# Causal mask of the attention scores: from TensorE's products to additions on VectorE

## The chip, the cores and the metric

The kernel runs on one core of a Trainium2 chip. Its time is the device time of one execution in microseconds (us). The kernel before took 1857.26 us, the median of three executions (1856.35, 1857.26 and 1864.93 us).

The engines are TensorE (PE in the profile, with its weight loads as PEld), VectorE (DVE), ScalarE (ACT), GpSimd (POOL) and SyncE (SP, which issues the DMAs). TensorE writes its results to PSUM, which the kernel declares as 128 partitions of eight banks of 512 32-bit words.

## The reference, cut to what matters

The program is a small audio model: a patch embedding, causal attention, a mixture of four experts, a linear recurrence and a quantised feed-forward block, with a residual sum around each. The input is 8 batch elements of 376 tokens of 256 columns after the embedding. The change touches the attention alone:

```python
def _L0_attn_ref(x, Wq, Wk, Wv, Wo, bo):
    HEADS = 16
    DIM_HEAD = 64
    ...
    q = split_heads(x @ Wq)
    k = split_heads(x @ Wk)
    v = split_heads(x @ Wv)
    q = apply_rope(q)
    k = apply_rope(k)
    sim = jnp.einsum('bid,bjd->bij', q, k) * scale
    causal = jnp.tril(jnp.ones((t, t), dtype=bool))
    sim = jnp.where(causal[None], sim, -jnp.inf)
    attn = jax.nn.softmax(sim, axis=-1)
    out = jnp.einsum('bij,bjd->bid', attn, v)
    out = out.reshape(b, h, t, d).transpose(0, 2, 1, 3).reshape(b, t, h * d)
    return out @ Wo + bo
...
h = h + _L0_attn_ref(_layernorm(h, axis=-1), L0_attn_Wq, L0_attn_Wk, L0_attn_Wv, L0_attn_Wo, L0_attn_bo)
```

## The kernel before

The whole program is one launch with stages in blocks of their own: embedding (to about 82 us of the profile), attention (to about 940 us), then experts, recurrence and feed-forward. Each stage begins when all engines have left the one before, so what the attention stage takes longer or shorter moves everything behind it.

Attention works on one batch element after the other, and in each on eight pairs of heads. The 376 tokens are three tiles of rows: 0 and 1 with 128 rows, 2 with 120. Scores of tile i are computed only for the columns up to its own end (128, 256 and 376 columns), so a causal mask is needed only in the last block of each tile, on the diagonal. The scores of both heads of a pair lie in PSUM banks 0 and 1 (tiles 0 and 1) and 2 and 3 (tile 2). All products are made three times from a high and a low part of each factor.

The order of work on every engine is written out by hand, in the order of the code, and semaphores tie the engines together. One batch element is `begin` (the values v, and the output projection of the element before) and eight times `step`, one for each pair c. I call them the first to the eighth step of elements 0 to 7. In a step on TensorE (`step`, L736) come, in this order: turn of the even head, which transposes the probabilities and divides them by the row sum (L650); a projection for a later pair (L612); the scores of the next pair (L625 and L635); turn of the odd head; mix of the even head, probabilities times values (L667); a second projection; mix of the odd head. In the fourth to eighth step of elements 1 to 7 a piece of the routing of the element before is added (`route`, L727).

The mask on TensorE is L620 to L627: before the scores of a pair, for each tile, two halves and two heads, a product of a 64-row half of an identity matrix with the matching half of the mask table, in bf16. The sum is the mask block itself (-1e30 above the diagonal, 0 elsewhere), which opens the accumulation in PSUM; the score products then add to it (start=False).

What follows the scores on the other engines in a step:
- VectorE (`step`, L1137): turned_low of the even head (L1000, the low part of the transposed probabilities, which allows mix), a shuffle for the rotation of q or k (L977), `maxima` of the next pair (L979 to L986, negated row maxima of tiles 2, 0, 1, both heads at once), turned_low of the odd head, two `diagonals` (L988), a shuffle, out_low (L1005). In some steps routing work is added, `weigh` in the sixth, `choose` at the end of the seventh, `place_rows` in the eighth, and the addition of a bias to the residual at the end of the fifth.
- ScalarE (`step`, L872): turned_high of the even head (L832), a copy of the projection (L810), the exp of tile 2 of the even head, which waits for its maximum (L823), only then turned_high of the odd head, then the exps of tiles 0 and 1 and of the odd head, parts of q and k (L816), a copy, out_high. In the fourth and fifth step router_x (L857) stands behind turned_high of the odd head.
- GpSimd rotates q and k and makes their low part (L950, L952, L954, L923).

Mix of the odd head waits for the odd turned_low:

```python
pe.wait_ge(pt_ready, 16 * b + h + 1 + CR_PT)
```

and the scores of a pair wait until all exps of the pair before have read their banks (L619).

Of the kernel before, what the change touches and what calls it, by code (L numbers as in the profile page):

```python
# [19 lines left out]
BF16 = mybir.dt.bfloat16  # L20
# [377 lines left out]
def attention(nc, psum, h0_rows, x_dram, weights, a, consts, ident, x_slots, h_rows, onehot, where, shared, raw_w, w_in,  # L398
# [3 lines left out]
    with ctx:  # L402
# [25 lines left out]
        mask = sb("mask", [P, 2, P], BF16)  # L428
        ident_b = sb("ident_b", [P, 2, P], BF16)
        mask_f = sb("mask_f", [P, 2, P])  # L430
        ident_f = sb("ident_f", [P, 2, P])
# [41 lines left out]
        (tables_in, masks_made, resid_in, cleared, v_made, v_high, v_low, proj_made,  # L473
# [3 lines left out]
            "tables_in masks_made resid_in cleared v_made v_high v_low proj_made "  # L477
# [59 lines left out]
        with nc.Block(no_gpsimd_drain=True) as block:  # L537
            @block.sync
            def _(sp):
# [4 lines left out]
                sp.dma_start(mask_f[:], a["c_mask"]).then_inc(tables_in, 16)  # L544
                sp.dma_start(ident_f[:], a["c_ident_halves"]).then_inc(tables_in, 16)
# [36 lines left out]
            def _(pe):  # L582
# [34 lines left out]
                def scores(b, c):  # L617

                    pe.wait_ge(exp_made, 16 * b + 2 * c + CR_EXP)  # L619
                    for it in range(TILES):  # L620
                        ni = TILE_ROWS[it]
                        for half in range(2):
                            for par in range(2):
                                r = slice(HEAD * par, HEAD * (par + 1))
                                pe.matmul(score_bank(par, it)[:, P * it:P * it + ni], ident_b[r, half, 0:ni],  # L625
                                          mask[r, half, 0:ni], start=(it != 1 and half == 0), stop=False,
                                          skip_group_check=True)  # L627
                    pe.wait_ge(qk_ready, 16 * b + 2 * c + 2 + CR_QK)
                    for it in TILE_ORDER:
                        ni = TILE_ROWS[it]  # L630
                        nj = P * it + ni
                        for i, (hq, hk) in enumerate(three):
                            for par in range(2):
                                r = slice(HEAD * par, HEAD * (par + 1))
                                last = pe.matmul(score_bank(par, it), qk[hq][r, c % 2, 0, P * it:P * it + ni],  # L635
                                                 qk[hk][r, c % 2, 1, 0:nj], start=False, stop=(i == 2),
                                                 skip_group_check=True)
                        if it != 0:
                            last.then_inc(scores_made, 1)
# [145 lines left out]
                pe.wait_ge(masks_made, 2)  # L785
# [130 lines left out]
            def _(pool):  # L916
# [25 lines left out]
                pool.wait_ge(tables_in, 64)  # L942
# [21 lines left out]
            def _(dve):  # L964
# [14 lines left out]
                def maxima(b, c):  # L979
                    for it in TILE_ORDER:  # L980
                        ni = TILE_ROWS[it]
                        if it != 1:
                            dve.wait_ge(scores_made, 16 * b + 2 * c + (1 if it == 2 else 2) + CR_SCORES)
                        last = dve.tensor_reduce(neg_max[0:ni, :, it], both_scores(it), AX_X, ALU.max, negate=True)  # L984
# [183 lines left out]
                dve.wait_ge(tables_in, 64)  # L1168
                dve.tensor_copy(mask[:], mask_f[:]).then_inc(masks_made, 1)
                dve.tensor_copy(ident_b[:], ident_f[:]).then_inc(masks_made, 1)  # L1170
# [1091 lines left out]
def constants():  # L2262
# [24 lines left out]
    halves = lambda x: np.tile(x.reshape(2, HEAD, P).transpose(1, 0, 2), (2, 1, 1)).astype(np.float32)  # L2287
    return {"c_moe": moe, "c_ids": ids, "c_slots": slots, "c_before": before, "c_ident_halves": halves(np.eye(P)), "c_cos": cos, "c_sin": sin, "c_mask": halves(np.where(behind, NEG, 0.0)),
# [38 lines left out]
```

## Time and profile before

| | |
|---|---|
| median of three executions | 1857.26 us |
| the profiled execution | 1865.4 us |
| span in its profile | 1863.6 us |
| PE busy | 1553.8 us, 83% of the span |
| PEld busy | 1466.1 us, 79% |
| DVE busy | 1250.3 us, 67% |
| ACT busy | 993.4 us, 53% |
| POOL busy | 1005.9 us, 54% |
| mean granted TensorE clock | 0.915 of full speed |

The span runs from the first instruction of the profiled execution to its last, and the execution's own time is 1.8 us longer. Busy is the time in which an engine had at least one instruction under way; TensorE's matmuls are pipelined, so two that overlap do not count twice. A granted clock of 1.00 is TensorE's 2.4 GHz level, 0.50 its 1.2 GHz level. A line as L984 is line 984 of the kernel before; in the rows `expert_raw` is a piece of memory that several stages share, which in this stage holds the raw projections, the rotation table and the probabilities.

### The profile page before, as it was taken

What the parts mean: (1) busy time and instruction counts of PE and PEld (TensorE: products, weight loads), DVE (VectorE), ACT (ScalarE), POOL (GpSimd) and SP (SyncE); (2) the same over time, 40 slices, a digit from 0 to 9 for tenths busy, and PEclk for the clock granted to TensorE, in tenths of its full rate; (3) what the DMA queues carried; (4) which work ended last, traced back from release to release, by engine and by line L of the source; (5) the groups of instructions that cost most, each with busy time, mean ns of one, the idle gap of its engine ahead of it and who ended that gap; (6) DMA issues with size and microseconds to landing.
All of it is one profiled execution on the core that took longest, in us unless ns stands there. A gap on an engine that the chain in (4) does not pass through costs nothing. (4 is left out here: it accounts for less than half of the span.)

```text
span 1863.6 us, 31359 instructions
## 1 busy us (share of the span) xinstructions
PE 1553.8 (83%) x11301; PEld 1466.1 (79%) x11301; DVE 1250.3 (67%) x2526; ACT 993.4 (53%) x2138; POOL 1005.9 (54%) x814
## 2 busy tenths in 40 slices
PE   5389998989899999989759999999998846699229
PEld 4278998989898888989749999999997845598229
DVE  6547575766767676757535666666668749558896
ACT  5446564746556464747435455455554424349562
POOL 4368475776667575866346667767765633100000
PEclk8679998989899998989969999999999978799659
DMA  5590001000010101000046555555554431003223
GB/s 208 206 309 18 18 18 35 6 25 23 18 35 18 35 18 35 1 18 18 26 145 183 141 140 142 137 141 144 138 143 114 105 84 42 26 1 124 75 70 113
DMA packets 88242, 153.53 MB, mean 82 GB/s; under 512 B 8056, under 2 KB 65720, under 8 KB 87832
## 3 DMA queue, kind: packets, MB, share of 16 engines
q1 hardware_dynamic: 77576, 137.70, 23.8%
q0 software_dynamic: 10512, 13.83, 4.4%
q8 instruction: 90, 1.47, 0.3%
q14 instruction: 64, 0.52, 0.1%
HBM read 113.42 MB, written 51.45 MB: 88 GB/s over the span
## 5 line engine op out<-in xcount | busy, mean ns | idle before, releaser
L1523 POOL TENSOR_TENSOR expert_w_low<-expert_raw,expert_w_high 128x768 fp32r<-128x768 f32 x152 | 288.6, 1947 | 172.2 <-ACT expert_w_high L1348 167.1
L823 ACT ACTIVATE expert_raw<-psum,neg_max 120x376 f32<-120x376 f32 (+2 forms) x384 | 176.4, 482 | 140.6 <-DVE neg_max L984 140.5
L650 PE MATMUL psum<-diag,expert_raw 128*128 128x128 f32 (+2 forms) x1536 | 208.5, 288 | 26.5 <-DVE pt_low L1000 26.5
L650 PEld LDWEIGHTS psum<-diag,expert_raw 128*128 128x128 f32 (+2 forms) x1536 | 190.8, 199 | 33.2 <-issue 17.3
L923 POOL TENSOR_TENSOR qk_low<-rotated,qk_high 128x376 fp32r<-128x376 f32 x128 | 136.1, 1064 | 127.9 <-ACT qk_high L816 126.4
L1495 DVE TENSOR_TENSOR expert_act_low<-expert_act,expert_act_high 128x384 fp32r<-128x384 f32 x152 | 140.5, 924 | 79.9 <-ACT expert_act_high L1386 79.3
L1000 DVE TENSOR_TENSOR pt_low<-psum,pt_high 128x752 fp32r<-128x752 f32 x128 | 120.4, 940 | 106.3 <-ACT pt_high L832 106.1
L1386 ACT ACTIVATE expert_act_high<-expert_act 128x384 fp32r<-128x384 f32 x152 | 79.8, 525 | 205.5 <-DVE expert_act L1490 203.3
L950 POOL TENSOR_TENSOR rotated<-expert_raw 128x376 f32<-128x376 f32 x128 | 127.8, 999 | 94.9 <-ACT expert_raw L810 74.5
L1307 PE MATMUL psum<-slots_high,expert_w_high 128*128 128x384 f32 x608 | 159.6, 343 | 17.6 <-DVE expert_act L1490 16.5
L1307 PE MATMUL psum<-slots_low,expert_w_high 128*128 128x384 f32 x608 | 156.5, 338 | 0.0
L1307 PE MATMUL psum<-slots_high,expert_w_low 128*128 128x384 f32 x608 | 156.3, 338 | 0.0
L1318 PE MATMUL psum<-expert_w_high,expert_act_high 128*128 128x256 f32 x456 | 134.3, 295 | 11.7 <-ACT slot_out L1368 10.2
L952 POOL TENSOR_TENSOR expert_raw<-expert_raw,rope_sin 128x376 f32<-128x376 f32 x128 | 131.3, 1026 | 16.9 <-DVE expert_raw L977 16.9
L954 POOL TENSOR_TENSOR rotated<-rotated,expert_raw 128x376 f32<-128x376 f32 x128 | 130.9, 1023 | 10.0
L1348 ACT ACTIVATE expert_w_high<-expert_raw 128x768 fp32r<-128x768 f32 x152 | 126.5, 833 | 15.6 <-PEq L537 15.6
L1490 DVE TENSOR_TENSOR expert_act<-psum,silu 128x384 f32<-128x384 f32 x152 | 84.7, 557 | 67.3 <-ACT silu L1382 63.1
L1318 PE MATMUL psum<-expert_w_high,expert_act_low 128*128 128x256 f32 x456 | 128.4, 282 | 0.0
L1318 PE MATMUL psum<-expert_w_low,expert_act_high 128*128 128x256 f32 x456 | 128.4, 281 | 0.0
L832 ACT ACTIVATE pt_high<-psum 128x752 fp32r<-128x752 f32 x128 | 102.2, 798 | 47.1 <-PE psum L650 45.0
L667 PE MATMUL psum<-pt_high,v_high 128*128 128x376 f32 (+2 forms) x384 | 119.4, 311 | 3.8 <-DVE pt_low L1000 3.7
L1307 PEld LDWEIGHTS psum<-slots_high,expert_w_high 128*128 128x128 f32 x608 | 102.9, 191 | 24.3 <-issue 21.5
(294 smaller groups left out, 4451.5 us busy)
## 6 DMA issues: line engine op xcount, KB each, us to landing
expert_raw<-in_experts SPq DMA_DIRECT2D x152, 384.0 KB, 3.1
x_slots<-in_c_slots SPq DMA_DIRECT2D x4, 3168.0 KB, 28.6
slot_rows<-x_slots SPq DMA_DIRECT2D x19, 396.0 KB, 4.6
attn_x<-tok_xt SPq DMA_DIRECT2D x8, 752.0 KB, 4.0
x_parts<-attn_x SPq DMA_DIRECT2D x8, 752.0 KB, 4.6
up_spill<-held SPq DMA_DIRECT2D x5, 1128.0 KB, 5.0
held<-up_spill SPq DMA_DIRECT2D x5, 1128.0 KB, 6.6
patch<-in_patches SPq DMA_DIRECT2D x8, 376.0 KB, 8.1
```

What stands on the lines that cost most here:

```text
L650: last = pe.matmul(psum[0:nj, BANK_PT + bank, at:at + ni], probs[0:ni, h % 2, src:src + nj], diag[0:ni, h % 2, it, 0:ni], start=True, stop ...
L823: last = act.activation(probs[0:ni, h % 2, at:at + P * it + ni], score_bank(h % 2, it), ACT.Exp, bias=neg_max[0:ni, h % 2, it:it + 1], acc ...
L923: pool.tensor_tensor(qk[1][:, c % 2, k, :], rotated[:, k, :], qk[0][:, c % 2, k, :].bitcast(F32), ALU.subtract).then_inc(qk_ready, 1)
L950: pool.tensor_tensor(rotated[:, k, :], raw[:, k, :], cos[:], ALU.mult).then_inc(rope_made, 1)
L952: pool.tensor_tensor(swapped[:, k, :], swapped[:, k, :], sin[:], ALU.mult).then_inc(rope_made, 1)
L954: pool.tensor_tensor(rotated[:, k, :], rotated[:, k, :], swapped[:, k, :], ALU.add).then_inc(rot_made, 1)
L1000: dve.tensor_tensor(pt[1][:, h % 2, :, :], psum[:, BANK_PT:BANK_PT + 2, 0:TOK], pt[0][:, h % 2, :, :].bitcast(F32), ALU.subtract).then_inc ...
L1307: last = pe.matmul(psum[:, 2 * k + g % 2, 0:TILE_SLOTS], w[hw][:, f, at:at + P], xt[hx][:, i % 2, c, :], start=(n == c == 0), stop=(n == 2 ...
L1318: last = pe.matmul(psum[:, BANK_DOWN + s, 0:DIM], act_hl[ha][:, g % 2, P * s:P * (s + 1)], w[hw][:, f, 4 * P:4 * P + DIM], start=(n == f = ...
L1348: act.activation(w[0][:, g % RING, :], raw[:, g % RAW, :], ACT.Copy).then_inc(w_high, 1)
L1495: dve.tensor_tensor(act_hl[1][:, g % 2, :], act_f[:, g % 2, :], act_hl[0][:, g % 2, :].bitcast(F32), ALU.subtract).then_inc(low_made, 1)
L1523: pool.tensor_tensor(w[1][:, g % RING, :], raw[:, g % RAW, :], w[0][:, g % RING, :].bitcast(F32), ALU.subtract).then_inc(w_low, 1)
```

## The change

The masks leave TensorE. The two tables in bf16, the identity halves and the two casts that made them are gone; a table `causal` in 32-bit floats, 128 by 128 and once for each of two heads, is loaded in their place. The first score product of each tile now opens its accumulation (`start=(i == 0)`). On VectorE a new function `masked` adds the table to the diagonal block of each tile, in place in PSUM and for both heads at once: three TENSOR_TENSOR operations for each pair, over 2 x 120, 2 x 128 and 2 x 128 elements in a partition. `maxima` calls it first, and each maximum waits for its own tile's addition.

```diff
--- before.py
+++ after.py
@@ -425,10 +425,7 @@
         h = sb("attn_h", [P, T, DIM])
         rows = sb("x_rows", [P, T, ROW])
         xt = sb("router_x", [P, 2, TOK])
-        mask = sb("mask", [P, 2, P], BF16)
-        ident_b = sb("ident_b", [P, 2, P], BF16)
-        mask_f = sb("mask_f", [P, 2, P])
-        ident_f = sb("ident_f", [P, 2, P])
+        causal = sb("causal", [P, 2, P])
         holder = sb("holder", [P, 2 * PAIRS])
         stats = sb("row_stats", [P, T, 6])
         moments = sb("row_moments", [P, T, 2])
@@ -541,8 +538,7 @@
                     sp.dma_start(x[:, b, :, :, :].bitcast(F32), x_dram[:, :, :, tokens_of(b)]).then_inc(x_loaded[b], 16)
                 sp.dma_start(cos[:], a["c_cos"]).then_inc(tables_in, 16)
                 sp.dma_start(sin[:], a["c_sin"]).then_inc(tables_in, 16)
-                sp.dma_start(mask_f[:], a["c_mask"]).then_inc(tables_in, 16)
-                sp.dma_start(ident_f[:], a["c_ident_halves"]).then_inc(tables_in, 16)
+                sp.dma_start(causal[:], a["c_mask"]).then_inc(tables_in, 16)
                 sp.dma_start(bo[:], a["token_rows"][:, 3, :]).then_inc(params, 16)
                 sp.dma_start(w[:], a["L0_ffn_router_w"].rearrange("(c p) e -> p c e", p=P)).then_inc(params, 16)
                 sp.dma_start(bias[:], a["router_b"]).then_inc(params, 16)
@@ -617,14 +613,6 @@
                 def scores(b, c):
 
                     pe.wait_ge(exp_made, 16 * b + 2 * c + CR_EXP)
-                    for it in range(TILES):
-                        ni = TILE_ROWS[it]
-                        for half in range(2):
-                            for par in range(2):
-                                r = slice(HEAD * par, HEAD * (par + 1))
-                                pe.matmul(score_bank(par, it)[:, P * it:P * it + ni], ident_b[r, half, 0:ni],
-                                          mask[r, half, 0:ni], start=(it != 1 and half == 0), stop=False,
-                                          skip_group_check=True)
                     pe.wait_ge(qk_ready, 16 * b + 2 * c + 2 + CR_QK)
                     for it in TILE_ORDER:
                         ni = TILE_ROWS[it]
@@ -633,7 +621,7 @@
                             for par in range(2):
                                 r = slice(HEAD * par, HEAD * (par + 1))
                                 last = pe.matmul(score_bank(par, it), qk[hq][r, c % 2, 0, P * it:P * it + ni],
-                                                 qk[hk][r, c % 2, 1, 0:nj], start=False, stop=(i == 2),
+                                                 qk[hk][r, c % 2, 1, 0:nj], start=(i == 0), stop=(i == 2),
                                                  skip_group_check=True)
                         if it != 0:
                             last.then_inc(scores_made, 1)
@@ -782,7 +770,6 @@
 
                 for n in range(2 * LEAD):
                     project(0, n)
-                pe.wait_ge(masks_made, 2)
                 scores(0, 0)
                 pe.wait_ge(params, 16 * 7)
                 pe.wait_ge(routing, 2)
@@ -939,7 +926,7 @@
 
                 for part in range(2):
                     pool.memset(v[part].rearrange("p t c (k n) -> p (t c) k n", k=3)[:, :, 1, :].bitcast(F32), 0.0).then_inc(cleared, 1)
-                pool.wait_ge(tables_in, 64)
+                pool.wait_ge(tables_in, 48)
                 for b in range(BATCH):
                     for n in range(2 * PAIRS):
                         if n == 2 * LEAD and b >= 2:
@@ -976,11 +963,19 @@
                     dve.memset(holder[:, n % (2 * PAIRS):n % (2 * PAIRS) + 1], 0.0)
                     dve.stream_shuffle(swapped[:, n % 2, :], raw[:, n % 2, :], swap).then_inc(swap_made, 1)
 
-                def maxima(b, c):
+                def masked(b, c):
                     for it in TILE_ORDER:
                         ni = TILE_ROWS[it]
                         if it != 1:
                             dve.wait_ge(scores_made, 16 * b + 2 * c + (1 if it == 2 else 2) + CR_SCORES)
+                        block = both_scores(it)[:, :, P * it:P * it + ni]
+                        dve.tensor_tensor(block, block, causal[0:ni, :, 0:ni], ALU.add).then_inc(mask_added, 1)
+
+                def maxima(b, c):
+                    masked(b, c)
+                    for it in TILE_ORDER:
+                        ni = TILE_ROWS[it]
+                        dve.wait_ge(mask_added, 3 * (8 * b + c) + TILE_ORDER.index(it) + 1)
                         last = dve.tensor_reduce(neg_max[0:ni, :, it], both_scores(it), AX_X, ALU.max, negate=True)
                         if it != 0:
                             last.then_inc(max_made, 1)
@@ -1165,9 +1160,7 @@
                 dve.wait_ge(params, 16 * 7)
                 dve.tensor_copy(before[:], before_f[:]).then_inc(routing, 1)
                 dve.tensor_copy(base[:], const("region"))
-                dve.wait_ge(tables_in, 64)
-                dve.tensor_copy(mask[:], mask_f[:]).then_inc(masks_made, 1)
-                dve.tensor_copy(ident_b[:], ident_f[:]).then_inc(masks_made, 1)
+                dve.wait_ge(tables_in, 48)
                 for n in range(2 * LEAD):
                     swap_pairs(0, n)
                 maxima(0, 0)
...
-    halves = lambda x: np.tile(x.reshape(2, HEAD, P).transpose(1, 0, 2), (2, 1, 1)).astype(np.float32)
-    return {"c_moe": moe, "c_ids": ids, "c_slots": slots, "c_before": before, "c_ident_halves": halves(np.eye(P)), "c_cos": cos, "c_sin": sin, "c_mask": halves(np.where(behind, NEG, 0.0)),
+    return {"c_moe": moe, "c_ids": ids, "c_slots": slots, "c_before": before, "c_cos": cos, "c_sin": sin, "c_mask": np.stack([np.where(behind, NEG, 0.0)] * 2, axis=1).astype(np.float32),
```

The lines of the changed kernel lie up to 13 lower. On TensorE, around the scores of a pair in an ordinary step, this stood in the queue (psum<-mask,ident_b are the products of the mask; brackets name the semaphores that an instruction waits for):

```order
L612 MATMUL psum<-x_parts,L_attn_Wq_high 128x376 [waits raw_made]
L612 MATMUL psum<-x_parts,L_attn_Wq_high 128x376 x3
L612 MATMUL psum<-x_parts,L_attn_Wq_low 128x376 x2
L625 MATMUL psum<-mask,ident_b 128x128 [waits exp_made]
L625 MATMUL psum<-mask,ident_b 128x128 x7
L625 MATMUL psum<-mask,ident_b 120x120 x4
L635 MATMUL psum<-qk_high 120x376 [waits qk_ready]
```

And in the changed kernel:

```order
L608 MATMUL psum<-x_parts,L_attn_Wq_high 128x376 [waits raw_made]
L608 MATMUL psum<-x_parts,L_attn_Wq_high 128x376 x3
L608 MATMUL psum<-x_parts,L_attn_Wq_low 128x376 x2
L623 MATMUL psum<-qk_high 120x376 [waits qk_ready,exp_made]
L623 MATMUL psum<-qk_high 120x376
```

The twelve products are gone, and the first score product waits for both semaphores. On VectorE, from turned_low of the even head to turned_low of the odd head, the queue before was:

```order
L1000 TENSOR_TENSOR pt_low<-psum,pt_high 128x752 [waits pt_high]
L976 MEMSET holder 128x1 [waits raw_made]
L977 STREAM_SHUFFLE expert_raw<-expert_raw 128x376
L984 TENSOR_REDUCE neg_max<-psum 120x2 [waits scores_made]
L984 TENSOR_REDUCE neg_max<-psum 128x2 [waits scores_made]
L984 TENSOR_REDUCE neg_max<-psum 128x2
L1000 TENSOR_TENSOR pt_low<-psum,pt_high 128x752 [waits pt_high]
```

And in the changed kernel:

```order
L995 TENSOR_TENSOR pt_low<-psum,pt_high 128x752 [waits pt_high]
L963 MEMSET holder 128x1 [waits raw_made]
L964 STREAM_SHUFFLE expert_raw<-expert_raw 128x376
L972 TENSOR_TENSOR psum<-psum,causal 120x2x120 [waits scores_made]
L972 TENSOR_TENSOR psum<-psum,causal 128x2x128 [waits scores_made]
L972 TENSOR_TENSOR psum<-psum,causal 128x2x128
L979 TENSOR_REDUCE neg_max<-psum 120x2 [waits mask_added]
L979 TENSOR_REDUCE neg_max<-psum 128x2 [waits mask_added] x2
L995 TENSOR_TENSOR pt_low<-psum,pt_high 128x752 [waits pt_high]
```

Three additions stand ahead of the first maximum, and the second of them carries the wait for the scores of tiles 0 and 1, which before stood behind the first maximum. The queues of ScalarE and GpSimd hold the same instructions as before.

## Rows read from the trace of the kernel before

**Rows 1.** Windows view, attention stage: us, busy us (xcount) per engine, granted clock, DMA share, GB/s.

```profile
110.00:905.00 795.00, 742.97 (x6252) 696.99 (x6251) 538.82 (x1270) 467.33 (x1304) 541.11 (x536) 0.95 0.10 30
```

**Rows 2.** Groups by form, PE: the mask products: xcount | busy us, mean ns | idle.

```profile
L625 PE MATMUL psum<-mask,ident_b 64*128 64x128 bf16 x512 | 25.6, 220 | 0.0
...
L625 PE MATMUL psum<-mask,ident_b 64*120 64x120 bf16 x256 | 17.5, 215 | 0.0
```

**Rows 3.** Timeline, TensorE, an ordinary step: start us, us, what [idle before <-releaser].

```profile
142.81 0.59 PE L650 MATMUL psum<-diag,expert_raw 120*128 120x120 f32 x4
...
144.36 0.51 PE L625 MATMUL psum<-mask,ident_b 64*128 64x128 bf16 x12
144.68 0.41 PE L635 MATMUL psum<-qk_high 64*120 64x376 f32 x2
...
149.71 0.33 PE L667 MATMUL psum<-pt_high,v_high 128*128 128x376 f32 x1
...
150.85 1.54 PE L650 MATMUL psum<-diag,expert_raw 128*128 128x128 f32 x12
```

**Rows 4.** Timeline, VectorE, the same step.

```profile
144.27 0.94 DVE L1000 TENSOR_TENSOR pt_low<-psum,pt_high 128x752 fp32r<-128x752 f32 x1 [0.48 <-ACT pt_high L832]
...
145.14 0.58 DVE L977 STREAM_SHUFFLE expert_raw<-expert_raw 128x376 f32<-128x376 f32 x1
...
145.62 1.85 DVE L984 TENSOR_REDUCE neg_max<-psum 120x2 f32<-120x752 f32 x3
148.51 0.94 DVE L1000 TENSOR_TENSOR pt_low<-psum,pt_high 128x752 fp32r<-128x752 f32 x1 [1.04 <-ACT pt_high L832]
```

**Rows 5.** Timeline, ScalarE, the same step.

```profile
146.63 0.57 ACT L823 ACTIVATE expert_raw<-psum,neg_max 120x376 f32<-120x376 f32 x1 [1.68 <-DVE neg_max L984]
...
147.68 0.80 ACT L832 ACTIVATE pt_high<-psum 128x752 fp32r<-128x752 f32 x1 [0.38 <-PE psum L650]
```

**Rows 6.** Timeline, first step of batch element 7.

```profile
842.76 0.93 PE L650 MATMUL psum<-diag,expert_raw 120*128 120x120 f32 x7
...
846.91 1.28 ACT L823 ACT_TABLE_LOAD   x1 [1.66 <-DVE neg_max L984]
...
848.21 0.58 ACT L823 ACTIVATE expert_raw<-psum,neg_max 120x376 f32<-120x376 f32 x1
...
850.59 0.44 PE L667 MATMUL psum<-pt_high,v_high 128*128 128x376 f32 x1 [0.43 <-DVE pt_low L1000]
```

**Rows 7.** Groups by form, VectorE: what comes nearest to the new operation.

```profile
L1031 DVE TENSOR_TENSOR attn_h<-psum,resid 128x256 f32<-128x256 f32 x16 | 6.7, 425 | 31.1 <-PE psum L690 26.7 <-issue 4.3
...
L969 DVE MEMSET psum<- 128x752 f32 x1 | 0.7, 685 | 0.2 <-issue 0.2
```

**Rows 8.** Timeline, third and fourth step of batch element 3.

```profile
452.52 0.79 ACT L832 ACTIVATE pt_high<-psum 128x752 fp32r<-128x752 f32 x1
...
454.34 0.44 PE L667 MATMUL psum<-pt_high,v_high 128*128 128x376 f32 x1
...
460.36 0.57 ACT L823 ACTIVATE expert_raw<-psum,neg_max 120x376 f32<-120x376 f32 x1 [1.68 <-DVE neg_max L984]
...
461.68 0.80 ACT L832 ACTIVATE pt_high<-psum 128x752 fp32r<-128x752 f32 x1 [0.66 <-PE psum L650]
...
463.00 0.92 PE L612 MATMUL psum<-x_parts,L_attn_Wk_high 128*128 128x376 f32 x4 [0.20 <-ACT router_x L857]
```

**Rows 9.** Timeline, TensorE, sixth and seventh step of batch element 3.

```profile
484.01 0.92 PE L612 MATMUL psum<-x_parts,L_attn_Wk_high 128*128 128x376 f32 x4 [0.89 <-DVE odds L1055]
...
492.43 2.77 PE L650 MATMUL psum<-diag,expert_raw 128*128 128x128 f32 x12 [1.91 <-DVE pt_low L1000]
```

**Rows 10.** Timeline, ScalarE, eighth step of batch elements 1 and 2.

```profile
302.11 0.80 ACT L832 ACTIVATE pt_high<-psum 128x752 fp32r<-128x752 f32 x1 [0.96 <-PE psum L650]
...
404.28 0.79 ACT L832 ACTIVATE pt_high<-psum 128x752 fp32r<-128x752 f32 x1
```

**Rows 11.** Windows view: a stretch behind a wait.

```profile
492.40:495.20 2.80, 2.77 (x13) 2.80 (x14) 2.14 (x4) 0.67 (x2) 2.66 (x4) 0.52 0.03 6
```

More of the change, by code:

```diff
@@ L472, in attention @@
         x_loaded = [sem(f"attn_x_loaded{u}") for u in range(2)]
-        (tables_in, masks_made, resid_in, cleared, v_made, v_high, v_low, proj_made,
+        (tables_in, mask_added, resid_in, cleared, v_made, v_high, v_low, proj_made,
          raw_made, swap_made, rope_made, rot_made, qk_high, qk_ready, scores_made, max_made, exp_made,
@@ L476, in attention @@
             sem(n) for n in
-            "tables_in masks_made resid_in cleared v_made v_high v_low proj_made "
+            "tables_in mask_added resid_in cleared v_made v_high v_low proj_made "
             "raw_made swap_made rope_made rot_made qk_high qk_ready scores_made max_made exp_made "
```

## The prediction

> **What bounds the kernel now.** I read the windows view first. In the attention stage, which is all the change touches, TensorE is busy 743 of 795 us at a mean granted clock of 0.95 of full speed, VectorE 539, ScalarE 467, GpSimd 541 [rows 1]. By shares TensorE is the bound, and this view alone says that less work there is less time. The groups by form give the twelve products of a pair: 768 in all, 216 ns each, 43 us busy [rows 2]. But they overlap two by two and each other's loads: in the timeline the twelve start at 144.36 and the scores at 144.68, so a pair costs TensorE 0.32 us, and 64 pairs 20.5 us [rows 3].
>
> The timelines of one ordinary step on three engines tell what is late. I count a step from the end of its first turn (142.81 + 0.59 = 143.40) to the end of the next (150.85 + 1.54 = 152.39): 8.99 us, with TensorE without a gap [rows 3]. Beside it runs a second chain, through VectorE and ScalarE: turned_low and the shuffle, the three maxima from 145.62, the exp of tile 2 at 146.63, then turned_high of the odd head, its turned_low, and with that mix of the odd head on TensorE at 149.71 [rows 3 to 5]. The order of work ties exp of tile 2 ahead of turned_high of the odd head, so every delay of the first maximum runs down this chain. VectorE has 1.04 us of idle time before the odd turned_low [rows 4], yet ScalarE waits only 0.38 us for TensorE before turned_high [rows 5]. The idle time is behind the maxima's end; the slack that counts is on the way from the first maximum, and I measure it next.
>
> In the first step of a batch element a table load of ScalarE lies in that chain and lengthens it: 846.91 to 848.21, 1.30 us. There mix of the odd head does wait for pt_low, 0.43 us, and starts at 850.59, which is 6.90 us behind the turn's end at 843.69 [rows 6]. Without the load the chain takes 6.90 - 1.30 = 5.60 us. In an ordinary step mix starts 149.71 - 143.40 = 6.31 us behind the turn [rows 3]. So the chain has 0.71 us in hand, of which about 0.1 is lost when mix has waited (its first product takes 0.44 in place of 0.33 us [rows 3, 6]): 0.6 us.
>
> **The change, part by part.** TensorE loses the twelve products: -0.32 us a pair, where TensorE is what is late. The wait for exp_made moves to the first score product, whose wait for qk_ready it shares; nothing else is queued between.
>
> VectorE gains three adds a pair over 240 or 256 elements of PSUM, with the table from SBUF, written back to PSUM. They stand ahead of all three maxima, so the first maximum, which ran after tile 2's scores, now also waits for both other tiles' scores and all three adds. The scores are no delay: they would be all made by about 145.8, and VectorE reaches the second add at about 145.62 + 0.34 = 145.96. Nearest to an add is the TENSOR_TENSOR with one PSUM and one SBUF input, 256 elements: 425 ns [rows 7]. Its output lies in SBUF. A write to PSUM is shown only by a memset, 752 elements in 685 ns, 0.91 ns each [rows 7], so no slow port there. Neighbours on VectorE overlap: 144.27 + 0.94 ends 0.07 us after the shuffle starts, 145.14 + 0.58 ends 0.10 us after the maxima start [rows 4]; 0.085 on average. Three adds therefore delay the first maximum by A = 3 x (0.425 - 0.085) = 1.0 us. Lower end: at the memset's 0.91 ns an element and no fixed cost 752 elements take 0.7 us. Upper end: no overlap and 0.03 us for each wait, 1.37 us. I take 1.0, the row with the same operation and size. The waits on mask_added cost nothing at the first maximum: two adds lie between it and its own.
>
> The Trainium skill, VectorE: DVE Perf Modes, section "The DRAIN you can't avoid", says that the next operation does not start until the pipeline has emptied. That would be A = 3 x 0.425 = 1.28 us and a sum of 50.5 us by the formula below; VectorE starts operations before the ends of the ones ahead [rows 4], so this trace does not agree and I keep 1.0.
>
> What A costs depends on the step. There are eight in each of eight batch elements:
> - Ordinary ones, 13 (the second of elements 1 to 7, the first five and the last of element 0): slack 0.6, so A - 0.6 = 0.4 us each, and the products taken out bring nothing, since mix waits. 5.2 us.
> - The first of elements 1 to 7: the chain already sets it [rows 6]. 7 x 1.0.
> - The third of elements 1 to 7: turned_high of the odd head starts at 452.52 without a wait and mix follows pt_low at 454.34, 0.2 us of it unhurried at most [rows 8]. 7 x 1.0.
> - The fourth and fifth of elements 1 to 7: turned_high waited 0.66 us for the turn, at 461.68; by the exp at 460.36 + 0.59 it could have gone 0.73 earlier. Behind it router_x holds TensorE's projection for 0.20 us [rows 8]. A - 0.73 = 0.27, 14 times: 3.8 us.
> - The sixth, 8 of them: the bias added to the residual has made VectorE late, the projection waits 0.89 us for weigh behind the odd turned_low, and the turn of the seventh step 1.91 us for a chain over exps, qk_split and GpSimd [rows 9]. Both waits hang on the same maxima: one A, 8 x 1.0. The seventh costs nothing more.
> - The eighth of elements 1 to 6: choose has set it. ScalarE then waits 0.96 us for a turn at half clock, which hides A; in two of the six steps the turn is fast and the wait is missing [rows 10]. 2 x 1.0.
> - Element 7's last two steps have no projections: 0.7 each, 1.4. The first pair before the loop: 1.0.
> Sum: 5.2 + 7 + 7 + 3.8 + 8 + 2 + 1.4 + 1.0 = 35.4 us slower, or 54 x A - 18.6 in general. The two casts of the tables (0.3 us of VectorE) and one DMA of 128 KB go before the loop; there VectorE next waits for projections, so nothing. The profiled execution took 1865.4 us; it becomes 1900.8. It lies 8.1 us above the median of the three runs, 1857.26, as one of them does (1864.93); I forecast on the median: 1893 us.
>
> **Rivals.** (1) TensorE's clock falls in more places. It stood at 0.52, the 1.2 GHz level, right behind the 1.91 us wait of the seventh step [rows 9, 11], where twelve turn products took 2.77 us in place of 1.54 [rows 3, 9]. The first step's wait would grow from 0.43 to 0.43 + 0.32 + 1.0 = 1.75 us, near that. Mix and turn behind it, 2.68 us, become 2.68 x (2.77 / 1.54 - 1) = 2.1 longer, seven times: 15 us more, 1908. Against it: no wait below 1.8 us in such a step has had this effect [rows 6, 8]. [...]
> (2) The adds are cheap and hide. The formula crosses zero at A = 0.34, one third of the row's price. At that point it is no change; if VectorE hid all of it and TensorE alone set each step, 64 x 0.32 = 20.5 us go: 1837, faster. For it speaks TensorE's 743 of 795 us and VectorE's 1.04 us of idle time, a hair more than A. Against it: TensorE already waits for VectorE in three kinds of step [rows 6, 8, 9], and that the idle time lies behind the maxima.
> (3) The adds cost more, as 1.37 us or above, by PSUM written and read: 54 x 1.37 - 18.6 = 55, 1912.
> (4) The slack is larger than 0.6 because a step that got longer relieves GpSimd and ScalarE elsewhere: only the 3A of first, third and sixth steps count, 22 us: 1879.
>
> **Numbers.** The forecast 0.62, rival 1 0.15, rival 3 0.06, rival 4 0.09, no change (A near 0.34) 0.05, faster 0.03. Range: from A = 0.7, 1857 + 19 = 1876, to A = 1.37, 1912. A difference under 0.5% (9 us) is what a measurement of this kernel can't tell from none. Faster by more 0.03, within 0.05, slower 0.92.
>
> **What the changed profile should show.** No mask products; three adds a pair near 0.42 us each, starting where the maxima started; the first exp of a pair about 1.0 us later behind its turn; VectorE's idle time before the odd turned_low near nothing and TensorE waiting for pt_low at mix in almost every step, some 0.7 us of it in ordinary ones, over 1.5 us in first ones; steps of 9.4 us in place of 8.99. Adds well under 0.3 us, or ordinary steps at 8.7 us, would make the prediction wrong; a clock of 0.5 behind first steps would be rival 1.

## The result, and the profile after

| | before | after |
|---|---|---|
| median | 1860.92 us (4 runs, 1856.35 to 1864.93) | 1909.24 us (4 runs, 1907.98 to 1910.93) |
| profiled execution | 1865.4 us | 1910.93 us |
| span | 1863.6 us | 1909.1 us |
| PE busy | 1553.8 us | 1547.4 us |
| DVE busy | 1250.3 us | 1309.6 us |
| granted clock | 0.915 | 0.912 |

The ratio is 1.025, 95% interval 1.0214 to 1.0285: slower, as forecast, and 16 us above the 1893 us of the forecast. Profile against profile the loss is 45.5 us where 35.4 were forecast. The kernel before ran again beside the experiments, with medians of 1860.8, 1861.9 and 1861.6 us; the changed kernel did not, so a difference from its 1909.2 us rests on that agreement.

The windows view of the changed kernel, from its first scores to its last (columns as in [rows 1]):

```profile
109.10:944.00 834.90, 732.01 (x5455) 681.74 (x5454) 596.04 (x1455) 463.09 (x1303) 536.77 (x535) 0.95 0.09 29
```

The stretch from the first scores to the last is 791.0 us long before (111.28 to 902.32) and 834.9 after. TensorE has 762 products less in it and is busy 7.3 us less (739.3 before in that stretch), though the products alone were worth 20.5.

VectorE's groups by form, which answer to [rows 7]:

```profile
L972 DVE TENSOR_TENSOR psum<-psum,causal 128x256 f32<-128x256 f32 x128 | 48.0, 420 | 0.0
L972 DVE TENSOR_TENSOR psum<-psum,causal 120x240 f32<-120x240 f32 x64 | 26.3, 411 | 0.0
```

An add takes 420 ns, against the 425 of the row it was priced by. An ordinary step in the timelines of VectorE, ScalarE and TensorE, which answer to [rows 3 to 5]:

```profile
147.40 1.07 DVE L972 TENSOR_TENSOR psum<-psum,causal 120x240 f32<-120x240 f32 x3
148.38 1.86 DVE L979 TENSOR_REDUCE neg_max<-psum 120x2 f32<-120x752 f32 x3
150.79 0.94 DVE L995 TENSOR_TENSOR pt_low<-psum,pt_high 128x752 fp32r<-128x752 f32 x1 [0.56 <-ACT pt_high L819]
...
149.41 0.58 ACT L810 ACTIVATE expert_raw<-psum,neg_max 120x376 f32<-120x376 f32 x1 [2.67 <-DVE neg_max L979]
...
149.97 0.79 ACT L819 ACTIVATE pt_high<-psum 128x752 fp32r<-128x752 f32 x1
...
151.79 0.44 PE L655 MATMUL psum<-pt_high,v_high 128*128 128x376 f32 x1 [0.45 <-DVE pt_low L995]
153.03 1.54 PE L638 MATMUL psum<-diag,expert_raw 128*128 128x128 f32 x12
```

The first maximum starts 0.98 us behind the first add. ScalarE waits 2.67 us for it (1.68 before), and turned_high of the odd head follows the exp with no wait, where it had waited 0.38 us for the turn. Mix of the odd head waits 0.45 us. VectorE's idle time ahead of the odd turned_low is 0.56 us (1.04 before), where the prediction had it near nothing.

The first step of element 2 (ScalarE, then TensorE), to be read beside [rows 6], which show that of element 7, and then two windows of it:

```profile
339.08 1.28 ACT L810 ACT_TABLE_LOAD   x1 [2.65 <-DVE neg_max L979]
...
342.75 0.44 PE L655 MATMUL psum<-pt_high,v_high 128*128 128x376 f32 x1 [1.73 <-DVE pt_low L995]
...
344.72 2.42 PE L638 MATMUL psum<-diag,expert_raw 128*128 128x128 f32 x12
```

```profile
340.00:342.70 2.70, 1.03 (x6) 0.71 (x5) 0.94 (x2) 2.69 (x9) 0.00 (x0) 1.00 0.00 0
342.70:345.30 2.60, 2.55 (x12) 2.55 (x13) 1.94 (x7) 2.60 (x10) 0.92 (x1) 0.58 0.02 6
```

The wait is 1.73 us (0.43 before), and right behind it the granted clock is 0.58, mostly at the 1.2 GHz level: the twelve turn products take 2.42 us in place of 1.54. All seven first steps of elements 1 to 7 look so.

The waits of TensorE in 110 to 950 us (line, what it waited for: us in total, times, longest):

```profile
PE psum L638 <- DVE pt_low L995: 32.1, 23, 3.3
PE psum L655 <- DVE pt_low L995: 24.8, 28, 1.7
...
PE psum L608 <- DVE odds L1050: 12.7, 6, 2.1
PE psum L608 <- ACT router_x L844: 10.2, 14, 0.8
```

Mix of the odd head waits 28 times, in the ordinary, first and third steps and one other, and not in almost every step as the prediction had it. The wait for router_x grew from 0.20 to about 0.73 us, that for weigh from 0.89 [rows 9] to 2.1.

From here on a step is counted from the start of one pair's scores to that of the next. Step lengths in us, means over the elements, from the timeline of TensorE of each kernel (ordinary: five of element 0 and the second of elements 1 to 7; seventh and eighth together; what a kernel has more in the sixth it often has less in these, so the last two columns are read as a sum; each figure is good to about 0.02 us):

| kernel | median, us | ordinary x12 | first x7 | third x7 | fourth, fifth x13 | sixth x6 | seventh + eighth x6 |
|---|---|---|---|---|---|---|---|
| before | 1860.9 | 8.99 | 9.68 | 9.52 | 9.66 | 11.36 | 44.90 |
| after | 1909.2 | 9.39 | 12.27 | 10.61 | 9.88 | 12.32 | 44.87 |
| products and adds | 1910.5 | 9.63 | 11.60 | 10.61 | 10.12 | 13.10 | 44.18 |
| no mask | 1851.3 | 8.68 | 9.68 | 9.52 | 9.36 | 11.32 | 44.23 |
| adds doubled | 1992.1 | 10.35 | 13.98 | 12.05 | 10.85 | 14.36 | 46.82 |
| interleaved | 1878.5 | 9.19 | 10.14 | 9.97 | 9.42 | 11.80 | 45.50 |
| after, early load | 1889.1 | 9.39 | 9.40 | 10.60 | 9.88 | 13.05 | 44.17 |
| before, early load | 1856.9 | 8.99 | 8.99 | 9.52 | 9.66 | 11.36 | 44.46 |
| after, exchanged | 1882.8 | 8.97 | 10.01 | 10.30 | 9.92 | 11.67 | 45.84 |
| before, exchanged | 1882.2 | 8.99 | 10.31 | 9.93 | 10.21 | 11.37 | 45.06 |
| mixed | 1858.5 | 8.80 | 9.68 | 9.60 | 9.47 | 11.34 | 44.37 |
| mixed, early load | 1854.3 | 8.80 | 8.80 | 9.60 | 9.47 | 11.34 | 44.94 |
| the same, exchanged | 1868.4 | 8.80 | 8.80 | 10.09 | 10.02 | 11.34 | 44.98 |
| interleaved, early load, exchanged | 1877.9 | 8.98 | 8.88 | 10.44 | 9.92 | 11.82 | 45.51 |

### The profile page after: what moved, and what is told of

The parts are those of the page before. It is cut to its first block and busy times, and to the rows that moved or that the text cites. A ratio compares the mean times of both kernels' runs of the same rounds, so it can differ in the third digit from the quotient of the medians.

```text
span 1909.1 us, 30068 instructions
## 1 busy us (share of the span) xinstructions
PE 1547.4 (81%) x10533; PEld 1455.3 (76%) x10533; DVE 1309.6 (69%) x2716; ACT 990.3 (52%) x2138; POOL 1002.4 (53%) x814
## 5 line engine op out<-in xcount | busy, mean ns | idle before, releaser
L638 PE MATMUL psum<-diag,expert_raw 128*128 128x128 f32 (+2 forms) x1536 | 217.2, 296 | 32.1 <-DVE pt_low L995 32.1
L638 PEld LDWEIGHTS psum<-diag,expert_raw 128*128 128x128 f32 (+2 forms) x1536 | 199.5, 207 | 38.7 <-ACT expert_raw L797 20.8
L1300 PE MATMUL psum<-slots_high,expert_w_high 128*128 128x384 f32 x608 | 161.0, 346 | 16.6 <-DVE expert_act L1483 15.4
L655 PE MATMUL psum<-pt_low,v_high 128*128 128x376 f32 (+2 forms) x384 | 120.0, 312 | 0.0
```

The lines of the kernel that those rows point to most:

```text
L638: last = pe.matmul(psum[0:nj, BANK_PT + bank, at:at + ni], probs[0:ni, h % 2, src:src + nj], diag[0:ni, h % 2, it, 0:ni], start=True, stop ...
L655: last = pe.matmul(psum[:, BANK_O, P * j:TOK], v[hv][0:nj, j, c, HEAD * par:HEAD * par + P], pt[hp][0:nj, par, bank, col:col + n], start=( ...
L1300: last = pe.matmul(psum[:, 2 * k + g % 2, 0:TILE_SLOTS], w[hw][:, f, at:at + P], xt[hx][:, i % 2, c, :], start=(n == c == 0), stop=(n == 2 ...
```

## Experiments: is it the late first maximum?

**Products and adds both.** The twelve products of before stay, and the adds of the changed kernel stand in `maxima` as well.

```diff
 maxima(b, c) of before:
+    masked(b, c)      # the three adds of the changed kernel
```

> The twelve mask products per pair of heads stand as in the kernel before, and VectorE's three adds stand too (the mask is applied twice). My theory, that VectorE's late first maximum sets the step and TensorE has slack in it: the products cost nothing or little in the ordinary steps, which stay at the 9.39 us of the changed kernel, and the whole comes out near 1909 us, at most some 5 us above it. The rival, that both engines' work adds up on the path: the twelve products' 0.3 us or so in each of some 60 steps come back, near 1928 us.

1910.47 us, ratio to before 1.0263 (1.0248 to 1.0279). The total is the one that my theory gave, the ordinary step is not: it takes 9.63 us and not 9.39, so the products cost 0.24 of their 0.32 us though TensorE waits in every such step. The timelines (VectorE, TensorE) show why:

```profile
147.64 1.31 DVE L987 TENSOR_TENSOR psum<-psum,causal 120x240 f32<-120x240 f32 x3
148.86 1.86 DVE L994 TENSOR_REDUCE neg_max<-psum 120x2 f32<-120x752 f32 x3
...
146.38 0.51 PE L627 MATMUL psum<-mask,ident_b 64*128 64x128 bf16 x12
146.70 0.41 PE L637 MATMUL psum<-qk_high 64*120 64x376 f32 x2
...
147.86 0.28 PE L637 MATMUL psum<-qk_high,qk_low 64*128 64x256 f32 x2
```

The products stand ahead of the scores, and the adds, unlike the first maximum of before, wait for the last of them (147.86 + 0.28 = 148.14). The first maximum starts 1.22 us behind the first add in place of 0.98, and the difference is the 0.24 us. That the total is the same is luck: four of the seven first steps took 10.9 us in place of 12.3, because their clock stayed up, of which more at the end.

**No mask at all.** Neither products nor adds.

> Neither the mask products nor the adds: the causal mask is left out on the diagonal blocks, so the output is that of an unmasked diagonal. My theory: only the steps that TensorE sets gain the products' time: ordinary 8.99 to 8.67 us, fourth and fifth steps of an element by 0.3 us, the steps that wait for exps or for the router by nothing; together about 9 us less than before, near 1852 us. The rival, that TensorE's work sets every step: 20 us less than before, near 1840 us.

1851.26 us, 0.9951 (0.9937 to 0.9964), 9 us below before. Ordinary steps take 8.68 us, fourth and fifth 9.36, first and third as before. So 20.5 us of TensorE's work were worth 9, because only some 27 steps, the ordinary, fourth and fifth ones, were set by TensorE. That is the most that any handling of the mask could bring with the rest of the order as it is. Against this kernel the three adds cost 58 us.

**Adds doubled.** Each of the three adds is made twice.

```diff
 masked(b, c):
     for it in TILE_ORDER: add(it)
+    for it in TILE_ORDER: wait for mask_added; add(it)
```

> Each of the three adds is done twice (the mask is added twice), so the first maximum is late by about 2 us in place of 1. My theory: every us of delay costs 54 us, so near 1963 us, with the ordinary step at 10.4 us; if TensorE's clock falls in more steps than now, more than that. The rival, that the wait of the changed kernel is the shuffle's or the exps' own and not the adds': less than 20 us more, below 1930 us.

1992.08 us, 1.0704 (1.0688 to 1.072). The timeline of VectorE gives A = 150.88 - 148.92 = 1.96 us:

```profile
148.92 1.07 DVE L972 TENSOR_TENSOR psum<-psum,causal 120x240 f32<-120x240 f32 x3
149.90 1.07 DVE L977 TENSOR_TENSOR psum<-psum,causal 120x240 f32<-120x240 f32 x3
150.88 1.86 DVE L984 TENSOR_REDUCE neg_max<-psum 120x2 f32<-120x752 f32 x3
```

The ordinary step is 10.35 us, 0.96 more. The total is 29 us above my 1963, and the windows view of the stretch of scores shows where from:

```profile
109.20:1018.20 909.00, 755.14 (x5455) 702.48 (x5454) 656.10 (x1644) 463.17 (x1303) 535.57 (x535) 0.92 0.08 26
```

TensorE does the same 5455 instructions in 755.1 us where the changed kernel took 732.0, 23.1 us more, and the clock accounts for that: 755.1 x 0.92 and 732.0 x 0.95 are both 695. The stretch grew by 909.0 - 834.9 = 74.1 us; without the clock's part it is 51.0, and 54 x 0.98 is 53. As far as this sum goes the slope of the forecast holds; what it leaves out is the clock.

**Interleaved.** The same adds, the first directly ahead of the first maximum, the others behind it.

```diff
-    add(2); add(0); add(1); max(2); max(0); max(1)
+    add(2); max(2); add(0); add(1); max(0); max(1)
```

> The same three adds, in another order on VectorE: add of tile 2, maximum of tile 2, then add 0, add 1, maximum 0, maximum 1. So the first maximum, which the first exp waits for, is late by one add (0.4 us) and not by three (1.0 us). My theory (the delay of the first maximum is what costs): ordinary step 9.39 to about 8.8 or 8.9 us, first step of an element 12.27 to about 10.2 us since TensorE's wait there shrinks by 0.6 us and its clock then holds, total 1861 to 1870 us. Rival A (VectorE's added work costs the same wherever it stands): near 1909 us. Rival B (with the delay gone TensorE alone sets the steps): near 1840 us.

1878.54 us, 1.0092 (1.0077 to 1.0107): 31 of the 48 us come back with VectorE's work unchanged, which excludes both rivals. The total is still 8.5 us above the 1870 that ended my range. In element 0 the ordinary steps are 8.99 us. In the second step of elements 1 to 7 they are 9.36, which I had not expected. Timelines of ScalarE and TensorE in the second step of element 2, and last the same turn in the kernel before:

```profile
343.89 1.60 ACT L837 ACTIVATE x_rows<-attn_h,row_shift,row_rstd 128x256 f32<-128x256 f32 x3
345.38 0.81 ACT L819 ACTIVATE pt_high<-psum 128x752 fp32r<-128x752 f32 x1
...
347.31 1.45 PE L638 MATMUL psum<-diag,expert_raw 128*128 128x128 f32 x11 [0.61 <-DVE pt_low L999]
...
351.44 0.44 PE L655 MATMUL psum<-pt_high,v_high 128*128 128x376 f32 x1 [0.37 <-DVE pt_low L999]
...
346.90 1.56 PE L650 MATMUL psum<-diag,expert_raw 128*128 128x128 f32 x12 [0.35 <-DVE pt_low L1000]
```

There ScalarE scales the rows of the batch element before (x_rows, 1.60 us) ahead of the next turned_high. In the kernel before the next odd turn waited too, but 0.35 us; with the exps later it is 0.61, and mix waits another 0.37. That the later exps are the cause of both is read from the timelines; no run takes x_rows away. Against the kernel before, the seven second steps are 2.6 us longer together, the first and the third 3.2 each, and the sixth to eighth of elements 1 to 6 some 6; what holds these last was not taken apart.

## Experiments: the table load and the clock

**Early load.** A small Exp on a spare element stands in the first step of elements 1 to 7 ahead of the exp that waits.

```diff
     raw_copy(b, ahead)
+    if b and c == 0: act.activation(spare, consts[:, 0:1], ACT.Exp)
     exps(b, 2 * c + 2, (2,))
```

> The changed kernel, with one small Exp on a spare element put on ScalarE in the first step of elements 1 to 7, behind the copy of the raw scores, so that the load of the Exp table (1.28 us) runs while VectorE still adds and takes maxima. My theory: TensorE's wait of 1.73 us in that step goes nearly whole, its clock then holds at 1.00, and the step falls from 12.27 us to 9.4 to 9.7 us: seven times 2.6 to 2.9, some 19 us less, near 1890 us. The rival, that the clock's fall comes from something else than this wait (TensorE's work earlier in the step): only the wait goes, seven times 1.2 us, near 1901 us.

> The kernel before with the same small Exp ahead of the table load's place. My theory: its first step loses what it has over an ordinary one, 9.67 to about 9.0 us, seven times: 5 us less than before, near 1856 us. The rival, that the load was hidden there: no change.

On the changed kernel this gives 1889.08 us, 1.0149 (1.0116 to 1.0183), 20 us less; on the kernel before 1856.88, 0.9967 (0.9953 to 0.9982), 5 us less than the 1861.86 of the kernel before beside it. Both are as expected. ScalarE's and TensorE's timelines and the windows of the changed kernel with it:

```profile
332.51 1.28 ACT L867 ACT_TABLE_LOAD   x1
333.80 0.20 ACT L867 ACTIVATE spare<-consts 128x1 f32<-128x1 f32 x1
335.16 0.57 ACT L811 ACTIVATE expert_raw<-psum,neg_max 120x376 f32<-120x376 f32 x1 [1.15 <-DVE neg_max L982]
...
337.54 0.44 PE L656 MATMUL psum<-pt_high,v_high 128*128 128x376 f32 x1 [0.45 <-DVE pt_low L998]
...
338.79 1.54 PE L639 MATMUL psum<-diag,expert_raw 128*128 128x128 f32 x12
```

```profile
337.50:341.00 3.50, 3.46 (x26) 3.46 (x27) 2.48 (x8) 3.37 (x11) 1.70 (x2) 1.00 0.02 5
```

The first step is an ordinary one: 9.40 us, a wait of 0.45, clock 1.00, twelve turn products in 1.54 us. The load had cost 2.87 us a step, of which about 1.3 is the load and about 1.6 the clock. The fall of the clock needs this wait: what TensorE did earlier in the step is the same in both kernels.

## Experiments: ScalarE's order, and keeping some products

**Exchanged.** turned_high of the odd head goes ahead of the exp of tile 2, in the changed kernel and in the kernel before.

```diff
+    turned_high(b, 2 * c + 1)
     exps(b, 2 * c + 2, (2,))
-    turned_high(b, 2 * c + 1)
```

> The changed kernel with ScalarE's evacuation of the odd head's turned weights put ahead of the exp of the third tile, so ScalarE's exps reach back less far into the wait for the last turned block. My theory: if the chain maximum, exp, shuffle is the path, the ordinary step loses what ScalarE's turn had in it, 9.39 to about 9.1 us, and the whole comes to about 1895 us; if VectorE's own queue (adds, maxima, shuffles back to back) is the path, the ordinary step stays at 9.39 us and the whole within 5 us of 1909 us.

> The kernel before with that exchange on ScalarE alone. If the exchange pays only where the adds make the first maximum late, this is as before or slower (1861 to 1868 us), and the 26 us that it gave in the changed kernel belong to the evacuation that stood behind the late exp. If it is a gain of its own, whatever the mask does, this is some 10 us or more below before (1850 us or less).

1882.78 us on the changed kernel, 1.01 (1.0067 to 1.0133), and 1882.16 on the kernel before, 1.0106 (1.0089 to 1.0122). The same exchange takes 26 us from the one and adds 21 to the other. In the changed kernel it took turned_high out from behind a late exp: ordinary steps go from 9.39 to 8.97 us (8.85 in element 0), first steps from 12.27 to 10.01. In the kernel before the exp came in time and ScalarE lost by waiting for the turn instead: the fourth and fifth steps go from 9.66 to 10.21 us, the first from 9.68 to 10.31, the third from 9.52 to 9.93. Both totals missed what I had expected, the first by 12 us to the good (1895) and the second by 14 to the bad (1868 at most). So ScalarE's order carries the delay to TensorE, as the prediction says, but the order is the right one where the maximum is on time.

**Mixed.** The four products of tile 2, whose maximum is the first, stay on TensorE; tiles 0 and 1 are masked by VectorE behind that maximum.

```diff
-    for it in range(TILES): products of the mask
+    for it in (2,): products of the mask
     maxima:
-    max(2); max(0); max(1)
+    max(2); add(0); add(1); max(0); max(1)
```

> The mask of the third tile (whose maximum and exp come first) is added by TensorE's four products as before; the masks of the other two tiles by VectorE's adds, put behind the first maximum. My theory: the first maximum isn't late at all, TensorE has eight products fewer in a pair of heads, and two adds fit beside the first exp: ordinary step 8.99 to 8.8 us, first and third steps unchanged, in all 0 to 5 us less than before, 1856 to 1861 us. The rival, that VectorE's 0.8 us of adds cost the step wherever they stand: near 1895 us.

1858.50 us, 0.9982 (0.9967 to 0.9996). Ordinary steps take 8.80 us, fourth and fifth 9.47, and the first are unchanged. VectorE does two thirds of the change's adds and the kernel is no slower. Timelines of one ordinary step, VectorE and ScalarE:

```profile
152.99 0.92 DVE L984 TENSOR_REDUCE neg_max<-psum 120x2 f32<-120x752 f32 x1
153.83 0.75 DVE L988 TENSOR_TENSOR psum<-psum,causal 128x256 f32<-128x256 f32 x2
154.49 1.01 DVE L991 TENSOR_REDUCE neg_max<-psum 128x2 f32<-128x256 f32 x2
155.69 0.94 DVE L1006 TENSOR_TENSOR pt_low<-psum,pt_high 128x752 fp32r<-128x752 f32 x1 [0.19 <-ACT pt_high L834]
...
154.01 0.57 ACT L825 ACTIVATE expert_raw<-psum,neg_max 120x376 f32<-120x376 f32 x1 [1.68 <-DVE neg_max L984]
```

The exp waits 1.68 us for its maximum, as before [rows 5]. The two adds lie in VectorE's idle time, 1.04 us before [rows 4], 0.19 now.

**Combinations.** The mixed masks with the early load; that with the exchange; and all masks by VectorE with interleaved order, early load and exchange.

> The mixed masks (TensorE's products on the third tile, VectorE's adds behind the first maximum on the other two) together with the early load of the Exp table. My theory: the two gains are of different steps and add up: ordinary step 8.8 us, first step of an element 9.0 us or a little less in place of 9.68; in all 7 to 9 us less than before, near 1854 us. The rival, that TensorE's work sets the first step once the load is gone and the mixed masks give nothing more there, or that the later steps give the time back: 4 us less, near 1858 us.

> The same with ScalarE's evacuation of the odd head's turned weights ahead of the exp of the third tile. My theory: in the steps with a wait for the turned weights (third, fourth and fifth of an element) the evacuation no longer stands behind an exp that waits for a maximum: 0.1 to 0.3 us less in each of 21 steps; but the exp of the third tile comes later by as much as the evacuation takes (0.8 us), which the router's copy behind it passes on. 3 us less than without the exchange to 5 us more. If the exchange only pays where the first maximum is late, it is the latter.

> All masks by VectorE, with all three repairs: the first add directly ahead of the first maximum, the early load of the Exp table, and the evacuation ahead of the exp. My theory: what is left of the loss is what VectorE's queue holds back of the last turned weights (0.37 us in the second step with the interleaved order alone), and the first step at about 9.4: near the time before, 1856 to 1868 us. The rival, that the repairs took away the same wait and don't add up: 1872 us or more.

- Mixed with early load: 1854.34 us, 0.9955 (0.9942 to 0.9968), 7 us below the kernel before beside it. The gains add up: the first step takes 8.80 us.
- With the exchange: 1868.42, 1.0038 (1.0024 to 1.0053). It loses 14 us, some 11 of them in the third to fifth steps, where I had allowed 5.
- All by VectorE with three repairs: 1877.90, 1.0086 (1.0073 to 1.0099), no better than the interleaved order alone. The first and the ordinary steps are at 8.88 and 8.98, but the exchange gives it back in the third to fifth (10.44 and 9.92 against 9.97 and 9.42). My range ended at 1868 us, so the rival stands: the repairs do not add up. Interleaved with the early load and no exchange was not run.

## Why the prediction was right in kind and short in size

Its terms against the two profiles, in us:

| term | forecast | measured |
|---|---|---|
| ordinary, 13 x 0.40 | 5.2 | 5.3 |
| first of elements 1 to 7 | 7.0 | 18.1 (85.9 - 67.8) |
| third | 7.0 | 7.7 |
| fourth and fifth (13 measured, without element 7's fifth) | 3.8 | 2.8 |
| sixth (7 measured, without element 7's) | 8.0 | 6.8 |
| seventh and eighth of elements 1 to 6 | 2.0 | -0.2 |
| element 7, from its fifth step to its last turn | 1.4 | 1.0 |
| first pair before the loop (its turn at 123.92, then 124.90) | 1.0 | 1.0 |
| sum to the last turn (terms rounded) | 35.4 | 42.6 |

- A was 1.0 and is 0.98: the row with the same operation was the right one, and writing to PSUM adds nothing that shows. The Trainium skill (VectorE: DVE Perf Modes, section "The DRAIN you can't avoid") has the next operation start when the pipeline is empty, which would make it 1.28, and lets one that is not held start earlier. The second is what these rows show: the three adds take 1.07 us from first start to last end.
- The slack of 0.6 us was right: ordinary steps came out at 9.39 us. The prediction wrote that mix would wait "some 0.7 us" there. The step is indeed 0.71 us longer than without any mask (9.39 - 8.68), but the profile shows only 0.45 of it as wait at mix: mix starts 0.62 us later than it could, the product ahead is still under way for 0.17 of that, and mix's slower first product is the last tenth.
- The step that failed is the first one, in "7 x 1.0". The delay is right (the wait grew by 1.30 us, and 0.32 of products went), but the wait's end was not the end of its cost. The clock fell behind it, and mix and turn took 2.15 + 2.42 us in place of 1.41 + 1.54: 1.62 us more, 11.3 over seven steps. That is rival 1, with the mechanism and wait (1.75 us written, 1.73 measured) in the place it named, and a price of 15 for 11.3. Its chance of 0.15 was too low, and the argument against it weak: "no wait below 1.8 us in such a step has had this effect" rested on waits of at most 0.89 us [rows 6, 9]. The trace of before had more to say. In it the same turn of the seventh step waits 1.89 to 1.91 us in each of elements 1 to 6; three times the turn then took 2.77 to 2.86 us, and three times 1.55 to 1.63. So [rows 9] show one of two outcomes, and neither was sure for a wait of 1.75 us. Early load shows that the fall goes with this wait.
- The measured time lies in the forecast's range, but its upper end stood there for dearer adds (A = 1.37), and A came out at 0.98. That the range covers the clock's 11.3 us is luck.
- Rival 2, that the adds hide, is excluded by interleaving (same work, 31 us less) and by no mask (9 us at most to win). Rival 3 fell with A, rival 4 with the 9.39 us.
- The eighth step's 2 us did not come. Of the eight sixth steps that of element 7 grew by only 0.2 us: its last three steps have no projections, and the prediction took it for two.
- The first pair's 1.0 us is right by luck. In the changed kernel its first scores start 1.6 us earlier (109.12 against 110.70), and the products for v behind them, which wait for its exps, 0.57 us earlier (117.67 against 118.24). But TensorE had waited 3.25 us there in place of 1.47, the granted clock up to the turn was 0.76 in place of 1.00, and the products took 7.2 us in place of 5.7.
- The rest of the 45.5 us, some 3, arose behind attention (its last prefix product, the last of L723, moved by 42.6 us). No run settles why. The median lies 16.2 us above the forecast, 16.6 above it unrounded (1892.7): 10.1 us are this difference of the profiles, 45.5 - 35.4; the rest is that the profiled execution of before lay 8.1 us above the median I forecast on, and that of after only 1.7 above its own.

## What to carry to other kernels

Price an operation that is added by the delay of the first result that something waits for, not by the engine's idle share: the same three adds cost 48 us ahead of the first maximum, 18 with one of them ahead, and two of them nothing behind it (with eight of the twelve products gone). When a wait of TensorE grows to the length of one that has been followed by half clock, give the sum with the instructions behind it at half clock too, and look at every wait of that length in the trace, not at one. And work that is spared on a busy engine is worth only the steps that this engine sets, 9 of 20.5 us here.

## What the runs showed of the hardware

The granted clock does not go by the length of the wait alone. In the changed kernel all seven waits of 1.72 to 1.74 us at mix were followed by half clock. With products and adds, the same wait lasted 1.65 or 1.66 us; four times of seven the clock held and the turn took 1.53 or 1.54 us, three times it took 2.3 to 2.8. With doubled adds the waits of 1.35 to 1.54 us held it each time, those of 1.82 to 1.84 us held it six times of ten, and after all seven of 2.70 us mix or the turn was slow. Two of the ten, from that kernel's timeline of TensorE, mix with its wait and the turn behind it:

```profile
265.25 0.44 PE L655 MATMUL psum<-pt_high,v_high 128*128 128x376 f32 x1 [1.84 <-DVE pt_low L1000]
...
266.49 1.53 PE L638 MATMUL psum<-diag,expert_raw 128*128 128x128 f32 x12
...
382.23 0.44 PE L655 MATMUL psum<-pt_high,v_high 128*128 128x376 f32 x1 [1.82 <-DVE pt_low L1000]
...
383.70 2.83 PE L638 MATMUL psum<-diag,expert_raw 128*128 128x128 f32 x12
```

The longer wait is the one behind which the clock held. Longer ones held it too. In the changed kernel the sixth step's projection waits 2.11 to 2.13 us in elements 1 to 6, and up to the next wait the granted clock is 1.00 all six times. With doubled adds the same projection waits 3.09 us, and in the 3 us behind it the clock is 1.00 three times and 0.50 or 0.51 three times. The kernel before has both outcomes behind the 1.9 us of its seventh step. Its turn in element 4, beside that of element 3 in [rows 9], and the changed kernel's projection in element 3 with its window:

```profile
596.59 1.55 PE L650 MATMUL psum<-diag,expert_raw 128*128 128x128 f32 x12 [1.90 <-DVE pt_low L1000]
...
504.64 0.93 PE L608 MATMUL psum<-x_parts,L_attn_Wk_high 128*128 128x376 f32 x4 [2.11 <-DVE odds L1050]
...
504.60:513.00 8.40, 6.21 (x51) 5.80 (x51) 3.81 (x14) 3.88 (x13) 6.75 (x7) 1.00 0.01 2
```

So something besides the length decides, and no row here shows what.

After a wait, mix takes 1.41 us in place of 1.31 even at full clock, since its first product takes 0.44 us in place of 0.33. That is a tenth of a microsecond for each wait, beside the wait itself.
